# Zero products on TensorE ahead of the sums in the gathering passes and the sort

## The reference

```
x += elu(segment_sum(h[src] * attn[src], dst) @ weight)          # attn: softmax over the nodes, 4 heads
x += relu(concat(h, segment_sum(relu(concat(h[row], h[col]) @ W.T + b), row)) @ W.T + b)
x += normalised(gat(gat(gat(h))) @ Wp + bp)                      # three attention convolutions, 8, 8 and 1 heads
x += mlp(concat(h, segment_mean(mlp(concat(h[src], edge_attr)), dst), u))
# gat: e = leaky_relu(a_src[src] + a_dst[dst]); ex = exp(e - segment_max(e)); out = segment_sum(ex * h[src]) / segment_sum(ex)
```

## Time and profile before

| what | value |
|---|---|
| median of 3 runs | 18701.26 us |
| profiled execution, its own time | 18737.4 us |
| its span, first to last instruction | 18735.7 us |
| mean granted TensorE clock (1 is 2.4 GHz) | 0.641 |
| PE busy / weight loads | 8575.8 us (46%) x53552 / 6897.0 us (37%) x53552 |
| VectorE (DVE) / ScalarE (ACT) | 8502.4 us (45%) / 6300.5 us (34%) |
| GpSimd (POOL) | 10982.0 us (59%) |
| first pass, about | 0 to 2750 us of the span |
| sort | 3250 to 6550 |
| carried pass | 6550 to 7050 |
| attention passes | 7400 to 9950, 10200 to 12750, 13000 to 15550 |
| attribute pass | 15800 to 18400 |

### The profile page before, as it was taken

How to read it: one execution, slowest core, us unless ns; L and a number is a source line. 1 busy time by engine, 2 the same in 40 slices (tenths; PEclk the granted TensorE clock), 3 DMA queues, 4 the chain that set the end, 5 groups by cost and what they waited for, 6 DMA issues and landing times. The chain is left out here.

```text
span 18735.7 us, 223246 instructions
## 1 busy us (share of the span) xinstructions
PE 8575.8 (46%) x53552; PEld 6897.0 (37%) x53552; DVE 8502.4 (45%) x29626; ACT 6300.5 (34%) x14065; POOL 10982.0 (59%) x11633
## 2 busy tenths in 40 slices
PE   4555542555555485344443444443444442444444
PEld 2334331444444384333332333333333332222223
DVE  5444443444444483455554554554444443222222
ACT  3665551444444473222222222222111121222332
POOL 5666656444444474666666666666666664555554
PEclk7777775666666696566666565665555555777777
DMA  5444432111111193444443444444333332232322
GB/s 173 153 150 153 149 119 69 60 60 59 57 60 60 46 336 110 136 139 139 141 139 113 141 142 138 143 141 90 88 89 88 87 84 51 87 91 89 93 89 72
DMA packets 933243, 2072.50 MB, mean 111 GB/s; under 512 B 430639, under 2 KB 457222, under 8 KB 892039
## 3 DMA queue, kind: packets, MB, share of 16 engines
q1 hardware_dynamic: 492023, 1019.05, 15.9%
q0 software_dynamic: 348560, 524.22, 12.1%
q10 hardware_dynamic: 92240, 525.31, 7.1%
HBM read 1165.51 MB, written 931.04 MB: 112 GB/s over the span
## 5 line engine op out<-in xcount | busy, mean ns | idle before, releaser
L119 POOL DMA_INDIRECT eg_got<-gat_table,edge_rows x4983 | 4757.5, 955 | 2675.3 <-issue 1415.8
L119 POOL DMA_INDIRECT e_got<-table,edge_rows x3322 | 3144.8, 947 | 2232.2 <-issue 970.1
L1678 PE MATMUL eg_ps_sum<-eg_got,eg_equal 128*128 128x136 f32 (+1 forms) x9984 | 2278.3, 404 | 1340.9 <-ACT eg_equal L1809 1326.9
L1678 PEld LDWEIGHTS eg_ps_sum<-eg_got,eg_equal 128*128 128x128 f32 x9984 | 2169.6, 313 | 1401.6 <-ACT eg_outs L1693 1359.5
L124 POOL DMA_INDIRECT sorted_rows<-sort_rows,sort_dest x1661 | 1611.1, 970 | 1679.7 <-ACT sort_rows L1238 1177.7
L1693 ACT ACTIVATE eg_outs<-eg_ps_sum 128x544 f32<-128x544 f32 (+1 forms) x1248 | 680.3, 545 | 2938.8 <-DMA last<-e_outs 2551.3
L1108 DVE SCALAR_TENSOR_TENSOR feat<-sort_ps_bc,sort_num,sort_before 128x128 bf16<-128x128 f32 (+3 forms) x1664 | 817.0, 546 | 1081.6 <-remote 1012.2
L1782 DVE TENSOR_TENSOR eg_total<-eg_up,eg_ends_score 128x128 f32<-128x128 f32 (+1 forms) x312 | 89.6, 287 | 2641.1 <-remote 2349.3
L2175 DVE COPY e_x_t<-e_ps_x 96x512 f32<-96x512 f32 x416 | 284.2, 683 | 1916.3 <-DMA w_bias_b<-in_L_gnn_b1b 760.4
L2163 PE MATMUL e_ps_second<-e_h_t,w_w_mid 128*128 128x512 f32 x832 | 534.2, 728 | 1343.1 <-DVE e_run L2183 936.5
L704 PE MATMUL e_ps_count<-e_hot_lo,e_hot_hi 128*128 128x512 bf16 x1664 | 604.5, 502 | 1153.2 <-DVE e_hot_lo L549 689.0
(11 more groups left out here) (523 smaller groups left out, 22293.1 us busy)
## 6 DMA issues: line engine op xcount, KB each, us to landing
shares<-eg_outs ACTq DMA_DIRECT2D x208, 1152.0 KB
eg_equal_b<-equal_d SPq DMA_DIRECT2D x312, 512.0 KB
feat<-values SPq DMA_DIRECT2D x312, 448.0 KB
sums<-e_outs ACTq DMA_DIRECT2D x104, 1024.0 KB
values<-e_zeros_b SPq DMA_DIRECT2D x104, 768.0 KB
values_q<-e_zeros_b SPq DMA_DIRECT2D x104, 768.0 KB
sort_value<-values_q SPq DMA_DIRECT2D x104, 768.0 KB
e_value<-values SPq DMA_DIRECT2D x104, 768.0 KB
```

The costliest lines, as they stand in the source:

```text
L119: return e.indirect_dma_start(out, None, table, bass.IndirectOffsetOnAxis(ap=index, axis=0), **kw)
L1678: last_i = e.matmul(ps_sum[q % 2][:, i, 0:FG], equal[q % 4][:, i, :], got[k][:, t, :], start=True, stop=True)
```

## The change

A new method issues `n` bf16 products whose two operands are the first column of `iota_free` (it holds 0), spread to 128x128 and 128x512, so that the bank gets zeros. In four functions the wait on the bank's release is moved ahead of the waits on the data, and the zero products go between them, into the bank that the sums then write (they start anew, so the zeros are overwritten). The first pass, the sort and the attribute pass get six per quad, the attention passes eight.

```diff
--- before.py
+++ after.py
@@ -202,6 +202,12 @@
 
     def dram(self, name, shape, dt=F32):
         return self.nc.dram_tensor(name, shape, dt, kind="Internal").ap()
+
+    def busy(self, e, bank, n):
+
+        zero = self.iota_free[:, 0:1]
+        for i in range(n):
+            e.matmul(bank, zero.to_broadcast([P, P]), zero.to_broadcast([P, BANK]), start=True, stop=True)
 
     def constants(self):
         self.x = self.sb("x", [P, NT, D])
@@ -724,9 +730,10 @@
 
         def pe_sums(e, it, q):
             k, tiles = at(q)
+            e.wait_ge(copied.sem, copied.at(it, q - 1))
+            self.busy(e, ps_sum[q % 2][:, :, :].rearrange("p t e -> p (t e)"), 6)
             e.wait_ge(gathered[buf(k)].sem, arrived(gathered, it, k))
             e.wait_ge(equaled.sem, equaled.at(it, q + 1))
-            e.wait_ge(copied.sem, copied.at(it, q - 1))
             for i in range(QT):
                 t = tiles.start + i
                 last_i = e.matmul(ps_sum[q % 2][:, i, 0:D], equal[k % 2][:, t, :], got[buf(k)][:, t, :], start=True, stop=True)
@@ -1176,9 +1183,10 @@
             last.then_inc(updated.sem, 1)
 
         def pe_look(e, it, q):
+            e.wait_ge(look_read.sem, look_read.at(it, q - 1))
+            self.busy(e, ps_look[q % 2][:, :, :].rearrange("p t e -> p (t e)"), 6)
             e.wait_ge(tabled.sem, tabled.at(it, q))
             e.wait_ge(hotted_t.sem, hotted_t.at(it, q + 1))
-            e.wait_ge(look_read.sem, look_read.at(it, q - 1))
             for i in range(QT):
                 last = e.matmul(ps_look[q % 2][:, i, :], hot_t[q % 4][:, i, :], table[q % 4][:, :], start=True, stop=True)
             last.then_inc(looked.sem, 1)
@@ -1670,9 +1678,10 @@
 
         def pe_sum(e, it, q):
             k, tiles = at(q)
+            e.wait_ge(copied.sem, copied.at(it, q - 1))
+            self.busy(e, ps_sum[q % 2][:, :, :].rearrange("p t e -> p (t e)")[:, 0:BANK], 8)
             e.wait_ge(message.sem, message.at(it, k + 1))
             e.wait_ge(equaled.sem, equaled.at(it, q + 1))
-            e.wait_ge(copied.sem, copied.at(it, q - 1))
             for i in range(QT):
                 t = tiles.start + i
                 last_i = e.matmul(ps_sum[q % 2][:, i, 0:FG], equal[q % 4][:, i, :], got[k][:, t, :], start=True, stop=True)
@@ -2163,8 +2172,9 @@
             e.matmul(flat(ps_second[q % 2]), w_mid[:, :], flat(h_t[q % 4]), start=True, stop=True).then_inc(second.sem, 1)
 
         def pe_back(e, it, q):
+            e.wait_ge(copied.sem, copied.at(it, q - 1))
+            self.busy(e, flat(ps_back[q % 2]), 6)
             e.wait_ge(summed.sem, summed.at(it, q + 1))
-            e.wait_ge(copied.sem, copied.at(it, q - 1))
             for i in range(QT):
                 last_i = e.transpose(ps_back[q % 2][:, i, :], run[q % 4][:, i, :], self.ident[:, :])
             last_i.then_inc(back.sem, 1)
```

## The result

The changed kernel took 19,568.87 us (median of 4 runs, 19,534.65 to 19,579.42) against 18,693.25 (18,656.78 to 18,735.43): ratio 1.0463, interval 1.0444 to 1.0482. It is slower by 876 us, where 1,770 were forecast. The profiled executions lie 797 us apart (span 19,532.9 against 18,735.7).

A forecast was written before the change was run, and what follows sets the result against it. POOL's indirect DMAs, plus its standing for late TensorE signals, were taken to bound the gathering stages. First pass 160 + attention 860 + attributes 440 + sort 310 = 1770 us on 18,737.4, less 36 for the median: 20,470 us; range 18,700 to 22,200.

The forecast's parts named there:

- the added 64 instructions use up what is let through in a POOL run: Attention group: signals of the fourth quad and turned maxima become late too, POOL stops once more; 2.75 us a group.
- Attention, 860 forecast: Three attention passes: 0.043 us of POOL standing per TensorE instruction, x 64 = 2.75 us a group, x 312 = 860 us.
- 8 x 0.42 = 3.4 us there are hidden: Attention, first quad's eight zero products: covered because TensorE has the scores turned six us ahead of the late release.
- late signal: Gathering stages: TensorE's signals reach waiting engines late, 6 us after its work ended in attention, by an inferred in-flight instruction limit.
- Attributes, 440 forecast: Attribute pass: 0.068 us x 48 = 3.2 us; open steps up to 5.2; 4.2 us a group taken, 440 us.
- The sub-step: Attribute pass, open stretch: six products put 1.3 us on each quad, which takes 2.59 us at the full clock.
- Sort, 310 forecast: Sort: longer open steps and fewer steps before TensorE slows, less some for the clock: 3 us x 104 = 310 us.
- the crawl: Sort: after about a hundred instructions into a POOL run TensorE slows to 0.57 us each; zeros make it start after fewer real products.
- the term's two shares: Sort, per group: 2 us from 1.5 longer low-clock steps, and 1.2 us from 0.3 of a step left for after.
- Only by work in the open: Rival, chance 0.22: release depends on POOL's progress; attention and first pass hide all, attributes and sort cost 480 us, 19,180 us.
- the worst case: Rival, chance 0.12: two more POOL stands per attention group, 2300 us, with 1200 for the other stages, 22,200 us.
- Faster, by the clock: Rival, chance 0.09: zeros keep TensorE at 2.4 GHz, products on the path halve; 570 us gained, 18,150 us.

## Why the prediction was right and wrong

**The sign and the place** were right: slower, mostly in attention, more stands of POOL (627 gaps of over 0.7 us between two attention gathers, 358 before) and not longer ones (3.05 us on average, 3.45 before), a higher clock without a shorter chain (0.60 to 0.73 in the first attention pass). The period of an attention group was to be 26.6 us; the passes give 23.9 + 590/312 = 25.8.

**The step that failed** is the price put on "the added 64 instructions use up what is let through in a POOL run": the rate of 0.043 us of standing per TensorE instruction, taken from the stage's own ratio and multiplied by the instructions added. Three of the four terms rest on such a rate, first pass and attention in whole, attributes in part. The first pass got 48 instructions a group and was to lose 160 us by it; it lost 26. The attributes were to lose 440 and lost 16. A ratio of two averages (stand per instruction) is no price of one more instruction. Beside it the zeros' own time was put at nothing in attention. What the runs showed in its place: where POOL stands, the cost is the zeros' own time in front of the first quad's sums. A seventh of the products, at that place, makes 738 of 755 us; the same eight issued a wait earlier cost 24.

**Attention, 860 forecast, 590 measured.** The size came near by luck. What was dismissed as hidden ("8 x 0.42 = 3.4 us there are hidden", by six us of lead) is the larger part of the cost: once a late signal moves to another step the lead is gone, and the first quad's eight lie in the open at 3.47 us, less 0.9 that they give back. Where POOL stands in each group by design, that was 2.4 us a group; in the first measurement it is 590/312, 1.9 on average.

How much of the 590 is of this kind can be read from the two traces. The code says for each of POOL's gaps of over 0.7 us which quad's sums it waited for, and the records say when TensorE had ended them. Before, the gaps in attention sum to 1235 us: 259 with those sums unfinished, 976 after they were done, which is the late signal. In the changed kernel they sum to 1915: 708 unfinished and 1207 after. So two thirds of what was added (449 of 680 us, of which 81 are the usual 0.30 us of 269 more gaps) is work that TensorE had still to do; the first quad's zeros run in such gaps for 574 us, for 1 us or more in 220 of the 303 groups that can be told apart.

The other third (231 us) is late signals, and here the prediction's own step is to be seen. The gaps in which POOL waits for a fourth quad's sums went from 42 (59 us) to 210 (624 us), so those signals did become late and POOL did stop once more. But at the first quad's sums the time after they were done fell from 871 to 244 us: most of the lateness moved, and little was added. In the first pass it grew by 15 us (444 to 459). No run repeated the first conditions, so what makes a signal late, and whether the number of instructions does, stays open.

**Attributes, 440 forecast, 16 measured.** The sub-step was right to the digit: a quad in the open takes 3.90 us (17706.44 to 17710.34) where it took 2.59, the 1.3 us of six warm products:

```profile
17706.44 1.02 PE L2166 MATMUL e_ps_first<-e_x_t,w_w_first 96*128 96x512 f32 x2
...
17708.16 1.47 PE L210 MATMUL e_ps_back<-iota_free 128*128 128x512 bf16 x6
...
17710.34 1.02 PE L2166 MATMUL e_ps_first<-e_x_t,w_w_first 96*128 96x512 f32 x2
```

But the pass did not grow by it: POOL's idle time in it, 2666 - 1524 = 1142 us before, is 1156. Each quad in the open is longer, so other stretches must have become shorter. In POOL's gaps of over 0.7 us in this pass TensorE ran 192 us of zeros, but its other products took 324 us instead of 394 and it idled 189 us instead of 289. Why it idled less is open.

**Sort, 310 forecast, 140 measured.** This is the place where a number of instructions could show. The kernel before and the changed one, columns as in the earlier trace rows; POOL starts at 4809.55 and at 4876.12:

```profile
4814.00:4818.00 4.00, 1.62 (x17) 1.04 (x14) 1.81 (x12) 1.52 (x4) 3.08 (x4) 1.00 0.08 25
4818.00:4822.00 4.00, 1.22 (x5) 0.89 (x5) 0.48 (x4) 0.00 (x0) 3.08 (x4) 0.52 0.08 25
```

```profile
4874.00:4878.00 4.00, 4.00 (x51) 3.36 (x48) 3.86 (x21) 3.58 (x10) 1.57 (x2) 1.00 0.55 168
4878.00:4882.00 4.00, 3.97 (x43) 2.96 (x41) 3.58 (x22) 3.89 (x9) 3.08 (x4) 1.00 0.54 199
4882.00:4886.00 4.00, 0.58 (x4) 0.38 (x4) 0.00 (x0) 0.28 (x1) 3.08 (x4) 0.93 0.09 25
```

Before, 44 and 17 products pass behind POOL's start, and then the crawl; after, about half of 51 and then 43, in which zeros take the place of real ones. Over the 102 POOL runs of the sort, 55.3 products on average begin within 8 us of POOL's start before and 57.0 after, 9.3 of these zeros. So the crawl came after fewer real products, as forecast, but at 1.35 us a group (140 / 104), not 3. It also came at the same time: six us after POOL's start the products that begin in 2 us fall from 21.5 to 2.6 before and from 24.3 to 4.4 after, so a limit by number and one by time are not told apart. Nor is which of the term's two shares was too large: no later run had a crawl to test on.

**The rivals.** "Only by work in the open" gave 19,180, closer to the 19,569 measured than the 20,470 of the forecast, and named the right kind of cost, but mostly in the wrong stages: attributes and sort, none in attention. Two of the rivals' sums are off: 570 us under the median is 18,130, not 18,150, and 13 us a group for the three other stages is 1,350 us, not 1,200, which makes the worst case 22,350; the forecast doesn't depend on either. "Faster, by the clock" is answered: the clock rose in every pass, and gave 0.9 us for 3.2. Here the Trainium skill, page "TensorE: Matmul & The Clock Gate", section "Why this matters for your kernels", advises keeping the engine at work without gaps. The runs agree that filler raises the clock (0.692 with the waits only, 0.844 with the zeros, in the later conditions) and show its limit: where the engine isn't the bound it gives nothing (1.0023), and ahead of sums for which another engine stands it costs (755 us).

## What to carry to other kernels

Filler work belongs ahead of the wait that really ends last, where its engine idles anyway (the first quad's zeros cost 24 us there), and not merely ahead of the next wait in the code, when the one that ends last lies before it (738 us): ask of each place which engine stands while it runs. Cover (idle time that seems to hide added work) read from one execution is worth only as much as the condition that made it; before adding to an engine that others wait for, add up what lies between the last release and the one that stands. A count that one engine raises behind its issue of a DMA says nothing of when that DMA begins (14.1 us later here); the semaphore of the landed data does. And the price of an instruction is measured by adding one, not by dividing a stage's idle time by its count.

## What the runs showed that was not expected

The same kernel took 18,693 us in one set of conditions and 14,928, 14,924, 14,924, 14,922 and 14,929 in five later ones, at the same cost per gather. Nearly all of it is POOL standing: its gaps of over 0.7 us in the gathering passes and the sort are 3,631 us of the first trace, of whose span the later one is 3,807 us shorter, and 2 us of the later one. The sort, where TensorE crawls, has the largest part (its window is 3789 us against 2567). What causes these conditions (another chip, its software, its neighbours) no run here told. A kernel whose stages lean on a prompt release can lose 25% to them, and a change that costs 0.2% in one set of conditions cost 4.6% in the other. In the later ones the number of TensorE instructions showed no cost apart from their time.
